# Spreading the routing weights of two FFN items by two 64-row products in different halves of the array

## The reference, cut to what matters

```python
H, I, E, K = (128, 64, 32, 8)                      # 1024 tokens in all
aff = sigmoid(x @ Wr + br)
top_v, top_i = top_k(aff, K)
w_full = zeros((T, E)).at[arange(T)[:, None], top_i].set(top_v / (sum(top_v) + 1e-9))
shared = (silu(x @ Wg_s + bg_s) * (x @ Wu_s + bu_s)) @ Wd_s + bd_s
gate = silu(einsum('th,ehi->eti', x, Wg) + bg[:, None, :])
up = einsum('th,ehi->eti', x, Wu) + bu[:, None, :]
down = einsum('eti,eih->eth', gate * up, Wd) + bd[:, None, :]
routed = einsum('te,eth->th', w_full, down)
out = x1 + shared + routed                         # x is the layer norm of x1
```

## Time and profile before

| | us |
|---|---|
| time, median of 3 runs | 213.03 (212.35 to 213.05) |
| the profiled execution's own time | 212.95 |
| its span, first to last instruction | 211.1 |
| mean granted TensorE clock | 0.986 |

### The profile page before, as it was taken

How to read it: one execution, slowest core, us unless ns; L and a number is a source line. 1 busy time by engine, 2 the same in 40 slices (tenths; PEclk the granted TensorE clock), 3 DMA queues, 4 the chain that set the end, 5 groups by cost and what they waited for, 6 DMA issues and landing times.

```text
span 211.1 us, 4012 instructions
## 1 busy us (share of the span) xinstructions
PE 193.0 (91%) x1239; PEld 139.6 (66%) x1251; DVE 163.8 (78%) x377; ACT 140.7 (67%) x275; POOL 95.5 (45%) x149
## 2 busy tenths in 40 slices
PE   7967988998999999898998886999999999999993
PEld 2635755766766767665765654778888888887662
DVE  2889994667688987987666799675788878887882
ACT  3457776778789888787786754754676566555571
POOL 7799881242182657448455053244255332220020
PEclk9999999999999999999999999699999999999997
DMA  4365423222342234101111100000033000000003
GB/s 117 86 150 138 111 71 75 43 70 75 89 94 68 71 83 114 39 0 40 40 38 37 37 0 2 3 0 0 2 75 79 17 2 0 0 3 0 0 0 99
DMA packets 20433, 10.39 MB, mean 49 GB/s; under 512 B 11881, under 2 KB 18542, under 8 KB 20414
## 3 DMA queue, kind: packets, MB, share of 16 engines
q1 hardware_dynamic: 19290, 9.24, 17.7%
q0 software_dynamic: 672, 0.69, 1.3%
q10 hardware_dynamic: 452, 0.23, 0.5%
HBM read 4.51 MB, written 0.52 MB: 24 GB/s over the span
## 4 chain that ended last, share of the span: by engine, by line
PE 65%; DVE 12%; issue 8%; ACT 8%; POOL 4%; DMA 1%; POOLq 1%; DVEq 0%; ACTq 0%
PE psum L1282 12%; PE psum L1283 11%; PE psum L1284 11%; PE psum L1385 5%; PE psum L1613 3%; PE psum L1458 3%; PE psum L1470 3%; PE psum L1480 3%; PE psum L1440 2%; PE psum L1435 2%; PE psum L1384 2%; PE psum L1421 2%; PE psum L1405 2%; PE psum L1444 1%; PE psum L1463 1%
## 5 line engine op out<-in xcount | busy, mean ns | idle before, releaser
L869 ACT ACTIVATE gate<-psum,bias_cols 128x512 f32<-128x512 f32 (+2 forms) x35 | 23.5, 674 | 31.8 <-PE psum L1284 31.7
L756 ACT ACTIVATE probs<-psum 128x512 f32<-128x512 f32 x64 | 36.9, 598 | 2.8 <-PE psum L1440 1.4
L1225 DVE SCALAR_TENSOR_TENSOR gated<-psum,bias_cols,gate 128x512 f32<-128x512 f32 x32 | 24.0, 749 | 11.4 <-ACT gate L869 10.9
L607 POOL TENSOR_TENSOR w_ffn_lo<-w_ffn,w_ffn_hi 128x384 fp32r<-128x384 f32 x17 | 20.7, 1216 | 25.8 <-ACT w_ffn_hi L770 25.8
L1282 PE MATMUL psum<-xT_hi,w_ffn_hi 128*128 128x512 f32 x66 | 27.1, 410 | 0.0
L1283 PE MATMUL psum<-xT_lo,w_ffn_hi 128*128 128x512 f32 x66 | 26.5, 401 | 0.0
L1284 PE MATMUL psum<-xT_hi,w_ffn_lo 128*128 128x512 f32 x66 | 26.0, 394 | 0.0
L1385 PE MATMUL psum<-key_blocks,query_rows 96*128 96x512 f32 x48 | 23.0, 522 | 0.3 <-issue 0.3
L1238 DVE TENSOR_TENSOR hid<-gated,psum 128x512 f32<-128x512 f32 x32 | 21.8, 683 | 1.6 <-PE psum L1613 0.6
L665 POOL TENSOR_TENSOR hid_lo<-hid,hid_hi 128x512 fp32r<-128x512 f32 x9 | 11.6, 1293 | 24.5 <-ACT hid_hi L876 24.5
L631 POOL TENSOR_SCALAR_AFFINE_SELECT probs<-probs 128x512 f32<-128x512 f32 x16 | 10.2, 640 | 27.1 <-ACT probs L756 27.0
(11 more groups left out here) (179 smaller groups left out, 475.6 us busy)
## 6 DMA issues: line engine op xcount, KB each, us to landing
query_rows<-queries SPq DMA_DIRECT2D x46, 64.0 KB, 2.0
key_rows<-keys SPq DMA_DIRECT2D x39, 32.0 KB, 1.9
w_ffn<-in_L_ffn_Wg SPq DMA_DIRECT2D x16, 64.0 KB, 1.9
w_ffn<-in_L_ffn_Wu SPq DMA_DIRECT2D x16, 64.0 KB, 2.1
...
```

The costliest lines, as they stand in the source:

```text
L607: ins = pool.tensor_tensor(w_ffn_lo[:, k, :, :], w_ffn[:, k, :, :], w_ffn_hi[:, k, :, :].bitcast(F32), ALU.subtract).then_inc(ffn_lo, 1)
L756: act.activation(probs[:, i % 2, c, :], bank(B_ST + c % 2), ACT.Exp, scale=SCALE).then_inc(exp_done, 1)
L869: act.activation(gate[rows_of(n), n % 3, part], psum[of, B_GATE + n % 2, part], ACT.Silu, bias=bias_cols[of, BIAS_GATE + u:BIAS_GATE + u + ...
L1225: dve.scalar_tensor_tensor(out=gated[:, n % 3, :], in0=bank(B_UP + n % 2), scalar=bias_cols[:, BIAS_UP + u:BIAS_UP + u + 1], in1=gate[:, n ...
```

## The change

The routes are kept twice in `routeT` (rows 0 to 63 and again 64 to 127), and `spread` has its ones in all four quarters of rows. Each spread product takes 64 rows. `spread_after(n)` says whose spread products stand at item n: for an even item those of n and n+1, one on rows 0 to 63 and one on rows 64 to 127, into the two banks; they stand behind the down product of n-2, not ahead of it, and wait for hid(n-1). An even item followed by the shared unit (28 and 32) has its own alone, at the old place. GpSimd makes four selects instead of two for a block of `spread_f`, two in the old step and two in the next; its clearing of `route` and `b_down` goes. The shared down bias leaves `b_down` (now 64 rows): it becomes one more row of `bias_rows`, loaded ahead of the keys' placement, and ScalarE adds it as it copies the sums to `ffnT`.

```diff
--- before.py
+++ after.py
...
@@ -104,14 +106,14 @@
         w_r = sb("w_r", [P, EXPERTS])
         w_r_hi = sb("w_r_hi", [P, EXPERTS], F32R)
         w_r_lo = sb("w_r_lo", [P, EXPERTS], F32R)
-        bias_rows = sb("bias_rows", [2 * UNITS, P])
+        bias_rows = sb("bias_rows", [FFN_BIASES, P])
         qkc_bias = sb("qkc_bias", [4, C])
         bias_cols = sb("bias_cols", [P, BIAS_ROWS])
         b_wide = sb("b_wide", [P, 3, C])
         b_r = sb("b_r", [P, EXPERTS])
-        b_down = sb("b_down", [P, C])
-        b_down_hi = sb("b_down_hi", [P, C], F32R)
-        b_down_lo = sb("b_down_lo", [P, C], F32R)
+        b_down = sb("b_down", [2 * EXPERTS, C])
+        b_down_hi = sb("b_down_hi", [2 * EXPERTS, C], F32R)
+        b_down_lo = sb("b_down_lo", [2 * EXPERTS, C], F32R)
         w_ffn = sb("w_ffn", [P, SLOTS, 3, P])
         w_ffn_hi = sb("w_ffn_hi", [P, SLOTS, 3, P], F32R)
         w_ffn_lo = sb("w_ffn_lo", [P, SLOTS, 3, P], F32R)
...
@@ -378,6 +379,14 @@
 
             return slice(INNER if WORK[n][0] == SHARED else 0, P)
 
+        ROUTE_ROWS = (slice(0, 2 * EXPERTS), slice(2 * EXPERTS, P))
+
+        def spread_after(n):
+
+            if n % 2 or WORK[n][0] == SHARED:
+                return ()
+            return (n, n + 1) if WORK[n + 1][0] != SHARED else (n,)
+
         HALF = CHUNK // 2
         HALVES = (slice(0, HALF), slice(HALF, CHUNK))
         block = stack.enter_context(nc.Block())
@@ -483,6 +492,7 @@
                               w[name].rearrange("(p e) i -> p (e i)", e=2)).then_inc(in_small, 16)
             sp.dma_start(bias_rows[PAIRS:PAIRS + 1, 0:INNER], row(w["bg_s"])).then_inc(in_small, 16)
             sp.dma_start(bias_rows[BIAS_UP + PAIRS:BIAS_UP + UNITS, INNER:P], row(w["bu_s"])).then_inc(in_small, 16)
+            sp.dma_start(bias_rows[BIAS_DOWN:FFN_BIASES, :], row(w["bd_s"])).then_inc(in_small, 16)
 
             sp.wait_ge(rows_set, 1)
             sp.wait_ge(qkc_rounded, 1)
@@ -497,10 +507,8 @@
 
             sp.dma_start(w_qkv[:, 4, :], w["Wp"]).then_inc(in_w_p, 16)
             sp.dma_start(w_r[:, :], w["Wr"]).then_inc(in_router, 16)
-            sp.wait_ge(b_down_set, 1)
             sp.dma_start(b_down[0:EXPERTS, :], w["bd"]).then_inc(in_down_bias, 16)
             sp.dma_start(b_down[EXPERTS:2 * EXPERTS, :], w["bd"]).then_inc(in_down_bias, 16)
-            sp.dma_start(b_down[2 * EXPERTS:2 * EXPERTS + 1, :], row(w["bd_s"])).then_inc(in_down_bias, 16)
             sp.dma_start(b_wide[:, 2, :], row(w["bp"]).to_broadcast([P, C])).then_inc(in_bp, 16)
             sp.dma_start(b_r[:, :], row(w["br"]).to_broadcast([P, EXPERTS])).then_inc(in_router, 16)
             place_batch(sp, 2)
@@ -531,7 +539,6 @@
             chain(pool.memset(minus_half[:, :], -0.5))
             pool.memset(key_rows[:, :, :, :].bitcast(F32), -1.0).then_inc(rows_set, 1)
             pool.memset(bias_rows[:, :], 0.0).then_inc(bias_rows_set, 1)
-            pool.memset(b_down[:, :], 0.0).then_inc(b_down_set, 1)
 
             def first_rstd(k):
 
@@ -586,20 +593,22 @@
                     ins = pool.tensor_tensor(x_sb[:, t, :], x_sb[:, t, :], b_wide[:, 2, :], ALU.add)
                 ins.then_inc(have_x_bp, 1)
 
-            def make_spread(k):
-
-                if k:
-                    pool.wait_ge(spread_copied, k)
+            def make_spread(k, quarters):
+
                 body = spread_f[:, :, :].rearrange("p u (e i) -> p u e i", e=2)
-                chain(pool.memset(spread_f[:, :, :], 0.0))
-                for half in range(2):
+                if quarters[0] == 0:
+                    if k:
+                        pool.wait_ge(spread_copied, k)
+                    chain(pool.memset(spread_f[:, :, :], 0.0))
+                for quarter in quarters:
                     ins = pool.affine_select(out=body, in_=body, compare_op=ALU.not_equal, fill=1.0,
-                                             base=-EXPERTS * half - 2 * SPREAD_UNITS * k,
+                                             base=-EXPERTS * quarter - 2 * SPREAD_UNITS * k,
                                              pattern=[[-2, SPREAD_UNITS], [-1, 2], [0, INNER]],
                                              channel_multiplier=1)
-                    if half == 0:
+                    if quarter < 3:
                         chain(ins)
-                ins.then_inc(have_spread, 1)
+                if quarters[-1] == 3:
+                    ins.then_inc(have_spread, 1)
 
             def split_unit(u):
                 k = u % SLOTS
@@ -642,17 +651,15 @@
                     pool.wait_ge(selected, 2)
                     expand_ctx(3)
                     pool.wait_ge(pool_ckey_blocks_set, 2 * GROUP)
-                    chain(pool.memset(route[:, :, :, :], 0.0))
-                    pool.memset(route[:, :, :, 2 * EXPERTS:2 * EXPERTS + 1], 1.0).then_inc(zeroed, 1)
                 if i in (3, 5, 7, 9):
                     if i == 3:
                         pool.wait_ge(in_bp, 16)
                         pool.wait_ge(x_normed, TILES)
                     add_bp(i // 2 - 1)
-                if i < BATCH:
-                    pass
-                elif i % 2 and i // 2 - 2 < SPREADS:
-                    make_spread(i // 2 - 2)
+                if i % 2 and 0 <= i // 2 - 2 < SPREADS:
+                    make_spread(i // 2 - 2, (0, 1))
+                if i % 2 == 0 and 0 <= i // 2 - 3 < SPREADS:
+                    make_spread(i // 2 - 3, (2, 3))
                 if ROUND_STEP <= i < ROUND_STEP + SLOTS:
                     split_unit(i - ROUND_STEP)
             add_y(STEPS - 2)
@@ -817,7 +824,7 @@
                     act.copy(w_qkv_hi[:, 4, :], w_qkv[:, 4, :]).then_inc(w_qkv_rounded, 1)
                     act.wait_ge(in_router, 32)
                     copy_hi(w_r_hi[:, :], w_r[:, :], w_r_rounded)
-                    act.wait_ge(in_down_bias, 48)
+                    act.wait_ge(in_down_bias, 32)
                     copy_hi(b_down_hi[:, :], b_down[:, :], b_down_rounded)
                 if ROUND_STEP <= i < ROUND_STEP + SLOTS:
                     round_unit(i - ROUND_STEP)
@@ -881,7 +888,8 @@
                     round_unit(SPLIT_AT[n])
                 if n == CHUNK_DONE[0] + 3:
                     act.wait_ge(m_down, CHUNK_DONE[0] + 1)
-                    act.copy(ffnT[:, :], bank(6)).then_inc(ffnT_copied, 1)
+                    act.activation(ffnT[:, :], bank(6), ACT.Identity,
+                                   bias=bias_cols[:, BIAS_DOWN:FFN_BIASES]).then_inc(ffnT_copied, 1)
             for h, part in enumerate(HALVES):
                 act.wait_ge(last_hid, h + 1)
                 if h == 0:
@@ -891,7 +899,8 @@
             act.wait_ge(m_down, ITEMS)
             act.wait_ge(t_ffn, 1)
             for part in HALVES:
-                act.copy(ffnT[:, part], bank(7)[:, part]).then_inc(ffnT_copied, 1)
+                act.activation(ffnT[:, part], bank(7)[:, part], ACT.Identity,
+                               bias=bias_cols[:, BIAS_DOWN:FFN_BIASES]).then_inc(ffnT_copied, 1)
 
         @block.vector
         def _(dve):
@@ -1136,16 +1145,15 @@
                                             r_top[:, :].unsqueeze(2).to_broadcast([P, 2, EXPERTS]), ALU.mult))
                     if b >= 2:
                         dve.wait_ge(t_route, b - 1)
-                    if b == 0:
-                        dve.wait_ge(zeroed, 4)
-                    to = route[:, b % 2, :, :]
-                    chain(dve.tensor_copy(to[:, :, 0:EXPERTS].bitcast(F32R), affinity[:, :, :]))
-                    dve.tensor_tensor(to[:, :, EXPERTS:2 * EXPERTS], affinity[:, :, :], to[:, :, 0:EXPERTS],
+                    to = route[:, b % 2, :, :].rearrange("p t (r e) -> p t r e", r=2)
+                    twice = affinity[:, :, :].unsqueeze(2).to_broadcast([P, 2, 2, EXPERTS])
+                    chain(dve.tensor_copy(to[:, :, :, 0:EXPERTS].bitcast(F32R), twice))
+                    dve.tensor_tensor(to[:, :, :, EXPERTS:2 * EXPERTS], twice, to[:, :, :, 0:EXPERTS],
                                       ALU.subtract).then_inc(route_ready, 1)
 
             dve.wait_ge(t_ffn_bias, 1)
-            dve.tensor_copy(bias_cols[:, 0:2 * UNITS],
-                            psum[:, B_BIAS, GROUP:GROUP + 2 * UNITS]).then_inc(have_ffn_bias, 1)
+            dve.tensor_copy(bias_cols[:, 0:FFN_BIASES],
+                            psum[:, B_BIAS, GROUP:GROUP + FFN_BIASES]).then_inc(have_ffn_bias, 1)
             dve.wait_ge(have_mask, 1)
             expand(0)
             expand_ctx(0)
@@ -1350,9 +1358,9 @@
             pe.wait_ge(ck_split, 1)
             run_idle(3, B_CK)
             turn_x(1)
-            pe.wait_ge(in_small, 64)
-            pe.transpose(psum[:, B_BIAS, GROUP:GROUP + 2 * UNITS], bias_rows[:, :],
-                         ident[0:2 * UNITS, 0:2 * UNITS]).then_inc(t_ffn_bias, 1)
+            pe.wait_ge(in_small, 80)
+            pe.transpose(psum[:, B_BIAS, GROUP:GROUP + FFN_BIASES], bias_rows[:, :],
```

(31 more changed lines are left out.)

7 lines of the change are left out of this document (4 added, 3 removed).

## The result

The changed kernel takes 218.27 us (median of 4 executions, 217.03 to 221.19), the kernel before 213.04 (212.35 to 213.09). The ratio is 1.0234, with an interval of 1.0180 to 1.0288: slower by 5 us. The highest time belongs to an execution in a slower state (mean granted clock 0.968) and is not in the ratio. The profiled execution took 218.67 us around a span of 216.7, so it is 0.4 us above the median.

What follows compares the result with a forecast made beforehand. TensorE's stream was taken to bound the kernel after 140.7 us. Start, pairs, bias, singles, ffnT and attention summed to +3.7 us on 212.95, giving 216.6 us; own range 215.3 to 218, 8-in-10 range 214.8 to 219.4.

Steps and rivals of the forecast that it cites:

- in turn: Rival: the two halves of a pair don't overlap, 0.233 for each of eleven steady pairs, 219.2 us; chance 0.17.
- the sum: All terms from the start, pairs, biases, singles, ffnT and attention added: +3.7 us on 212.95, giving 216.6.
- The price of a change of shape: On TensorE, going into 64 rows and out again costs 0.39 us, about 0.19 each way.
- The overlap: On TensorE, a pair's two 64-row products run side by side, freeing one slot of 0.233 us; two items take 4.81.
- shape changes for nothing: Rival: changes of shape on TensorE are free and a pair costs one slot, 211.2 us; chance 0.07.
- The steady sum: TensorE's FFN stream from gate(7): ten pairs 1.55, pair 30 0.25, bias 0.39, single 28 0.39, single 32 0.3, ffnT 0.2.
- single 28: The unpaired 64-row spread product of item 28, before a shared unit, costs one excursion: +0.39 us.
- single 32: The unpaired spread product ahead of gate(33), a little absorbed by ScalarE: +0.3 us, between 0 and 0.39.
- ffnT: At the end, two ScalarE copies become ACTIVATEs with a bias: +0.2 us, no table load taken.
- The start: FFN's start: spread(4) behind down(2) delays hid(4) and the route; gate(7) 0.5 us later, bounds -0.5 and +1.5.
- The attention: Added GpSimd selects fill a waiting gap; with the DMA and wider route copies, +0.1 us, 0 to +0.5.
- The start decides: Rival: slipping hid(4) idles TensorE around 139 and the clock falls a second time, 218.3 us; chance 0.08.

Runs made afterwards that it cites:

- the first experiment: The kernel before with every spread product on rows 0 to 63 alone, at its old place, none paired: 222.89 us, ratio 1.0485.
- the joined kernel: The changed kernel with the pairs at items 2 and 8 directly behind the two down-bias products: 218.55 us, 216.61 at full clock.
- the two kernels with 128 rows: The kernel before with paired 128-row spread products behind the down product: 214.14 us; the same with items 4 and 5 ahead of down(2): 212.80 us.

## Why the prediction was right, and where not

**Right: direction and range.** 216.6 was forecast, 214.8 to 219.4; 218.27 came. That is outside the forecast's own range of 215.3 to 218, and inside the wide one only because this reached up to the case *in turn*, which did not occur: there the range held by luck. Of the 1.7 us by which the forecast is low, none is in the reason that it gave for the loss. At full clock on both sides the change costs 217.03 - 212.4 = 4.6 where the sum had 3.7, so 0.9 is in the sum; the other 0.8 lies in where the low-clock stretches fell.

**The price of a change of shape: right.** 0.39 us for both ways was read off one down product on 64 rows, three matmuls. The first experiment gives 0.40 for a single matmul, the joined excursion 0.39. What the Trainium skill states (TensorEngine Tiling (Array Packing), Key Properties: changing the mode drains the array) agrees with it.

**The overlap: right.** 3 ns between the starts, a period of 4.81 us for two items (4.81 forecast), 5.07 with both on the same rows (5.04 forecast). The rival *in turn* is refuted by the period, the rival *shape changes for nothing* by the first experiment. This second rival would be what the Trainium skill's advice to pack makes of it (TensorE: Matmul & The Clock Gate, Why this matters for your kernels; its row is on slices of 32 partitions, here they are 64). The gap between the starts, at most 4 ns there, is 3 ns in this trace, but the 0.40 around the pair is there too.

**The steady sum: right.** From hid(7) to the end the forecast has 1.55 + 0.25 + 0.39 + 0.39 + 0.3 + 0.2 = 3.08, the lag gives 5.6 - 2.67 = 2.93. In detail: pairs 0.16 each (0.155 forecast), items 8 and 9 0.63 (0.155 + 0.39 = 0.55), single 28 0.27 (0.39), items 30 and 31 0.26 (0.25), single 32 0.32 (0.3). Some of this detail is placement and not shape: in the kernel with pairs of 128 rows the lag falls by 0.09 at single 28 and rises by 0.18 at items 30 and 31. Without it they are 0.36 and 0.08.

**ffnT: right in kind, small in size.** There is no table load:

```profile
207.35 0.69 ACT L891 ACTIVATE ffnT<-psum,bias_cols 128x512 f32<-128x512 f32 x1
...
208.29 0.83 ACT L876 ACTIVATE gate<-psum,bias_cols 64x256 f32<-64x256 f32 x2 [0.24 <-PE psum L1292]
...
212.46 0.84 ACT L902 ACTIVATE ffnT<-psum,bias_cols 128x256 f32<-128x256 f32 x2 [1.97 <-PE psum L1292]
```

Two ACTIVATEs take 0.84 us where two copies took 0.75, and the lag is 5.59 at hid(33) and 5.6 at the end. The term was 0.2 and measures 0.1 at most. ScalarE's gate of the last item comes at 208.29 behind 0.24 us of waiting for TensorE, so the 0.32 of single 32 was not absorbed.

**The start: the number right, its way not.** The rows that answer:

```profile
137.04 0.51 PE L1610 MATMUL psum<-routeT,spread 64*128 64x512 f32 x2
...
137.76 0.69 DVE L1246 TENSOR_TENSOR hid<-gated,psum 128x512 f32<-128x512 f32 x1 [1.18 <-PE psum L1610]
...
139.75 1.28 POOL L672 TENSOR_TENSOR hid_lo<-hid,hid_hi 128x512 fp32r<-128x512 f32 x1 [2.92 <-ACT hid_hi L883]
...
140.02 1.09 DVE L1140 SCALAR_TENSOR_TENSOR affinity<-not_top,affinity 128x64 f32<-128x64 f32 x1
...
141.94 0.29 DVE L1151 TENSOR_TENSOR route<-affinity,route 128x128 f32<-128x128 f32 x1
...
142.38 0.41 PE L1537 MATMUL psum<-ident,route 128*128 128x128 f32 x2 [1.85 <-DVE route L1151]
...
144.54 0.50 PE L1290 MATMUL psum<-xT_hi,w_ffn_hi 128*128 128x512 f32 x1
```

Take off the 2.36 us that the attention had brought. The pair starts at 134.68, hid(4) at 135.40, the route is done at 139.87 (139.8 in the step), down(4) follows at 140.97, and gate(7) starts at 142.18, where the step had 142.2 and before 141.73. By this count the term of 0.5 measures 0.45. But hid(4) is only 0.3 us later than before, not 1.2, since the clock is full here and was low before. In place of that slip the router's chain met a collision that no step had: 1.09 us for the affinity product beside GpSimd's hid_lo of 139.75, where the same instruction takes 0.22 in the kernel before (at 137.35). TensorE waits 1.85 us for the route. That the number came out is luck: a low stretch in the kernel before and a collision in the changed one happen to leave 0.45. With the same clock on both sides the start costs about 0.9 us, by the profile of the joined kernel, and that the place of one pair is worth about 1.0 is shown by the two kernels with 128 rows; in the changed kernel itself it is not shown.

**The attention: the step that failed.** "I put +0.1 on all, 0 to +0.5" measures 2.36 us in the profiled execution, of which 1.4 is the low-clock stretch, and 0.94 at full clock. At full clock the parts 0.94, 0.9 and 2.9 make 4.7, and the executions without a low stretch differ by 217.03 - 212.4 = 4.6. The step had asked whether GpSimd would be late with its own work, 1.49 us into a gap of 1.33, and on that it was almost right. It had not asked what VectorE does while GpSimd works. The text had named "a change of more than 0.5 us before 113" as what would show the prediction wrong; it was there. The trace of the kernel before held the evidence (124.46 and 130.16, above): one line, one shape, 0.16 us and 1.24. I had read lines for their mean durations and not for the difference between their shortest and longest.

**The clock.** *The start decides*, with a second low stretch, did not come about: the clock was full in the start. The stretch of 3.41 us came at 93 us, just behind TensorE's wait of 1.29 us for o_norm. That the one caused the other is not shown: the profile of the joined kernel has the same wait (1.30 us, until 92.23) and no low stretch. So where the stretch falls, and whether it comes, stays open. One of 3.41 us is worth 0.5 to 1.1 us in the kernel before and 0.8 to 1.6 in the changed one (217.87 and 218.67 against 217.03), and 10.24 us of it some 2.5 (220.3 against 217.74). The rival had put one at 1.7.
